# Group statistics of the last image on ScalarE, and three later places in a hand-ordered hypergraph convolution

## The reference

```python
def reference(x, fc_w, fc_b, dist_w, bn_gamma, bn_beta):      # x: (4, 128, 32, 32)
    v = gn(x, G=32, eps=1e-5)                 # group norm: groups of 4 channels, over 4 x 1024 values
    x_flat = v.reshape(B, C, N).transpose(0, 2, 1)            # N = 1024 points of C = 128
    emb = einsum('bnc,ec->bne', x_flat, dist_w)               # 32 wide
    d2 = sq[:, :, None] + sq[:, None, :] - 2.0 * einsum('bne,bme->bnm', emb, emb)
    dist = sqrt(clip(d2, 0.0))
    idx = top_k(-dist, 24)                                    # the 24 nearest points of each point
    adj = knn_mask & (dist <= 10.0) | eye(N)
    X_lin = x_flat @ fc_w.T + fc_b
    Dv, De = sum(adj, axis=2), sum(adj, axis=1)
    out = ((adj / De) @ adj.T / Dv) @ X_lin + x_flat
    o = batch_norm(out) * bn_gamma + bn_beta                  # mean and variance over all four images
    return x + o * sigmoid(o)
```

## Time and profile before

| | |
|---|---|
| median of 3 runs | 178.0 us (177.37 to 181.69) |
| the profiled execution | 177.34 us |
| its span, first to last instruction | 175.6 us |
| granted TensorE clock, mean | 0.97 of 2.4 GHz |
| busy: PE, VectorE, ScalarE, GpSimd | 153.0, 147.6, 108.2, 83.2 us |

### The profile page before, as it was taken

How to read it: one execution, slowest core, us unless ns; L and a number is a source line. 1 busy time by engine, 2 the same in 40 slices (tenths; PEclk the granted TensorE clock), 3 DMA queues, 4 the chain that set the end, 5 groups by cost and what they waited for, 6 DMA issues and landing times.

```text
span 175.6 us, 4086 instructions
## 1 busy us (share of the span) xinstructions
PE 153.0 (87%) x1255; PEld 99.0 (56%) x1257; DVE 147.6 (84%) x888; ACT 108.2 (62%) x200; POOL 83.2 (47%) x104
## 2 busy tenths in 40 slices
PE   7787999979997999899999999999987999998000
PEld 2223543446464772666668746766745888988000
DVE  0667989989999899998999999299989983599782
ACT  1245849999869858995546878257874333090290
POOL 2001309909995745457143989370019575740100
PEclk9999999999999999999999999999999999999855
DMA  6821000043705355046523225391509469600057
GB/s 192 270 92 2 0 2 4 1 52 72 118 7 120 36 90 121 6 95 147 121 37 88 62 63 122 119 93 32 120 0 95 91 181 100 145 4 0 2 201 277
DMA packets 41482, 14.83 MB, mean 84 GB/s; under 512 B 38736, under 2 KB 39656, under 8 KB 41456
## 3 DMA queue, kind: packets, MB, share of 16 engines
q1 hardware_dynamic: 40592, 14.14, 38.3%
q10 hardware_dynamic: 864, 0.40, 1.0%
HBM read 4.02 MB, written 2.13 MB: 35 GB/s over the span
## 4 chain that ended last, share of the span: by engine, by line
PE 67%; ACT 15%; issue 6%; DVE 5%; POOL 4%; ACTq 0%; POOLq 0%; DVEq 0%
PE pt L442 24%; PE pg L412 19%; PE po L467 12%; ACT key L619 4%; ACT H L628 3%; PE po L375 3%; PE pt L495 3%; ACT left L573 2%; PE po L399 2%; POOL wide L759 2%; DVE xn L1080 2%; ACT xn L708 1%; PE po L386 1%; ACT right L579 1%; PE pg L399 1%
## 5 line engine op out<-in xcount | busy, mean ns | idle before, releaser
L867 DVE MAX8 cand<-key 128x8 f32<-128x64 f32 x512 | 81.0, 210 | 1.5 <-ACT key L619 1.2
L442 PEld LDWEIGHTS pt<-xp,H 128*128 128x128 bf16 x768 | 44.4, 97 | 16.3 <-issue 13.9
L442 PE MATMUL pt<-xp,H 128*128 128x128 bf16 (+1 forms) x768 | 48.8, 220 | 0.9 <-DVEq L927 0.6
L759 POOL CAST wide<-HT 128x1024 fp32r<-128x1024 bf16 x31 | 31.4, 1040 | 36.1 <-PE po L467 26.9
L619 ACT ACTIVATE key<-pg 128x512 f32<-128x512 f32 x64 | 34.5, 591 | 22.3 <-PE pg L412 21.9
L412 PE MATMUL pg<-right,left 64*128 64x512 f32 x128 | 41.0, 641 | 4.0 <-ACT key L619 3.1
L628 ACT ACTIVATE H<-key,bound 128x1024 bf16<-128x1024 f32 x32 | 36.8, 1149 | 10.5 <-DVE bound L905 6.8
L467 PE MATMUL po<-wide,tp 128*128 128x512 f32 x96 | 25.4, 406 | 1.6 <-POOL tp L750 1.2
L412 PEld LDWEIGHTS pg<-right,left 64*128 64x128 f32 x128 | 12.7, 184 | 14.7 <-ACT key L619 7.6
L467 PEld LDWEIGHTS po<-wide,tp 128*128 128x128 f32 x96 | 17.1, 189 | 5.6 <-POOL tp L750 1.7
L882 DVE MAX8 top<-cand 128x8 f32<-128x128 f32 x32 | 9.3, 292 | 4.2 <-DVE cand L867 3.1
(11 more groups left out here) (96 smaller groups left out, 170.6 us busy)
## 6 DMA issues: line engine op xcount, KB each, us to landing
dvb<-inv_rows SPq DMA_DIRECT2D x3, 512.0 KB, 4.0
out<-xn SPq DMA_DIRECT2D x6, 256.0 KB, 2.2
x_sb<-x SPq DMA_DIRECT2D x1, 1024.0 KB, 6.2
x_sb<-x SPq DMA_DIRECT2D x1, 512.0 KB, 3.6
HT<-H SPq DMA_TRANSPOSE x32, 2.8
out<-xn SPq DMA_DIRECT2D x4, 128.0 KB, 2.2
x_sb<-x ACTq DMA_DIRECT2D x1, 256.0 KB, 3.2
x_sb<-x SPq DMA_DIRECT2D x1, 256.0 KB, 3.4
```

The source lines that it names most:

```text
L442: mm = pe.matmul(pt[:, j // T_BLOCKS, at:at + wide], lhs, x_cols(b, t, q, wide), start=(t == 0 and j % T_BLOCKS == 0 and q == 0), stop=(t ...
L759: pool.tensor_copy(wide[:, t // TH, :, t % TH * P:(t % TH + 1) * P], HT[:, k % HTS, :, :]).then_inc(s["widened"], 1)
L867: ins = dve.max(cand[:, k % 2, c, :], key[:, k % KEYS, c * CHUNK:(c + 1) * CHUNK])
```

## The change

- VectorE no longer takes image 3's statistics. ACT makes them by running sums: one Copy of the image with a sum, put behind its fourth key drain, and, after the key drain of step 0, one Square with the negative mean as bias and a sum. GpSimd scales the sums to mean and variance (`own_mean`, `own_variance`), three small operations ahead of its loop.
- The group means of images 2 and 3 move on PE from before the loop to step 2 and on VectorE from behind search 0 to behind search 3. The variances move on PE from step 1 to step 4 and on VectorE from behind search 2 to behind search 4; GpSimd's inverse and the normalisation of image 2 move from step 3 to step 4.
- Image 2's tiles 20 to 23 are widened at step 28 and no longer at steps 25 to 27.
- On ACT `operands(b, 1)` stands behind the step's key drain and no longer ahead of it.

```diff
-    [{7: (0, 1), 8: (2, 3), 9: (4, 5), 10: (6,), 11: (7,)}, {6: (0, 1), 7: (2, 3)}]
+    [{7: (0, 1), 8: (2, 3), 12: (4, 5, 6, 7)}, {6: (0, 1), 7: (2, 3)}]
...
@@ tensor engine
-            group_means(2, 2, B)
             keep_busy(3)
...
-                    if k == 1:
+                    if k == 2:
+                        pe.wait_ge(s["own_stat"], 3)
+                        group_means(2, 2, B)
+                    if k == 4:
                         group_variances(2, 2, B)
...
@@ scalar engine
             drain_key(0, 3)
+            act.wait_ge(s["x_in23"], 16)
+            act.activation(work[:, :], x_sb[:, B - 1, :], ACT.Copy, accum_out=own_sum[:, 0:1]).then_inc(s["own_sum"], 1)
             for b in range(B):
...
-                    if k - 2 in EMB_STEPS:
-                        operands(EMB_STEPS[k - 2], 1)
                     if b > 0 and t == SCALE_STEPS[b] + 1:
                         copy_inverse(b - 1)
                     if k + AHEAD < ALL:
                         drain_key((k + AHEAD) // TILES, (k + AHEAD) % TILES)
+                    if k - 2 in EMB_STEPS:
+                        operands(EMB_STEPS[k - 2], 1)
+                    if k == 0:
+                        act.wait_ge(s["own_stat"], 1)
+                        act.wait_ge(s["own_sum"], 1)
+                        act.activation(work[:, :], x_sb[:, B - 1, :], ACT.Square, bias=own_nm[:, :],
+                                       accum_out=own_sum[:, 1:2]).then_inc(s["own_sum"], 1)
...
@@ gpsimd
+            def own_mean(b):
+                pool.wait_ge(s["own_sum"], 1)
+                pool.tensor_scalar(own_nm[:, :], own_sum[:, 0:1], -1.0 / N, None, ALU.mult).then_inc(s["own_stat"], 1)
+                pool.tensor_scalar(gn_mv[:, b, 0:1], own_sum[:, 0:1], 1.0 / N, None, ALU.mult).then_inc(s["own_stat"], 1)
+
+            def own_variance(b):
+                pool.wait_ge(s["own_sum"], 2)
+                pool.tensor_scalar(gn_mv[:, b, 1:2], own_sum[:, 1:2], 1.0 / N, None, ALU.mult).then_inc(s["own_stat"], 1)
...
+            own_mean(B - 1)
+            own_variance(B - 1)
...
-                    if k == 3:
+                    if k == 4:
                         group_inverse()
...
@@ vector engine
-            group_stats(2, 3)
+            third_stats = group_stats(2, 3)
             candidates(0, range(CHUNKS))
             group_inverse(1, 1, 2)
-            dve.wait_ge(s["step"], group_stats(3, B))
-            group_moments(2, B)
+            dve.wait_ge(s["step"], third_stats)
+            group_moments(2, 3)
...
                     search(k)
-                    if k == 0:
+                    if k == 3:
                         group_scale(2, 2, B)
-                    if k == 2:
+                    if k == 4:
                         dve.wait_ge(s["gvar"], 3)
                         dve.tensor_scalar(gn_sd[:, 2:B], g_sums[2][:, B:B + 2], GN_EPS, None, ALU.add).then_inc(s["gvar_in"], 1)
```

More of the change, by code:

```diff
@@ L123, in build @@
         gn_mv = sb("gn_mv", [P, B, 2])
+        own_sum = sb("own_sum", [P, 2])
+        own_nm = sb("own_nm", [P, 1])
         gn_dm = sb("gn_dm", [P, B])
@@ L174, in build @@
         misc = ps("misc", [P, HALF])
-        names = ("const_in d_in w_in x_in0 x_in1 x_in23 out_done setup ones_cols gstat gmean gdm gvar gsd gscale "
+        names = ("const_in d_in w_in x_in0 x_in1 x_in23 out_done setup ones_cols gstat own_stat own_sum gmean gdm gvar gsd gscale "
                  "xn0_ready xn_ready filled drained po_filled po_drained e_sq n_filled l_made r_made norm_out "
```

## The result

The changed kernel is slower: 182.3 us (182.2 to 182.7) against 177.4 to 178.0 for the kernel before beside it, ratio 1.027 with a 95% interval of 1.025 to 1.029. That is outside the forecast range of 176.5 to 180.9. The profiled execution took 182.34 us and its span is 180.5, against 177.34 and 175.6 before, so the traces have to account for 4.9 to 5.0 us.

A forecast was written before the change was run, and what follows sets the result against it. PE and VectorE, both busy, meet at step 13, where VectorE is later by a few tenths. 177.34 + 2.8 (lag) - 0.34 (covered wait) - 0.6 (tail) = 179.2, plus 0.2 gives 179.4 us; range 176.5 to 180.9.

The forecast's parts named there:

- VectorE's gain: VectorE before search 5: two BN_STATS of 1.27 us together leave, but none of the gain outlives a wait.
- the slack of 3.4 us at the flag: Near 113.56 us VectorE waits 3.45 us for PE's flag; this is VectorE's slack and gives PE nothing back.
- the tail: End of kernel: PE's 1.24 us wait for t's low part goes, of which 0.6 us is gained, 0 at worst.
- GpSimd's normalisation of image 2: Comes later with the variances, done about 41.3 us, before the embedding at 44.35 needs it; costed at nothing.
- Step 4 starts when ACT has drained a key tile: PE's step 4, at 36.17 us in the earlier trace: its start was taken to follow ACT's key drain.
- Together 1.16 - 0.88 - 0.28 = 0.0 at best ... I take 0.1: ACT's chain before step 4: Square adds 1.16, left leaves 0.88, means leave 0.28; 0.1 us late taken.
- The release, taken at 1.0 us: VectorE after the variances: adding epsilon and releasing tiles 0 and 1 takes 1.0 us, bounds 0.6 and 1.45.
- my 2.8: Search 5 on VectorE starts 2.8 us late (2.1 to 3.5), and this lag runs on to step 13.
- 0.34 us back: Behind step 13's scatter, PE's 0.34 us wait for ACT's copy of t is covered, leaving PE 2.46 us late.
- the third rival: The stall at step 13 costs PE its clock; scatter and gather take twice as long, 3.65 more, 182.8 us; chance 0.10.
- One pays for the other: Image 2's left behind the drain takes 0.88 of PE's 1.1 us wait; the Square makes PE up to 1.16 late.
- The second rival: VectorE's work sets the pace, so 1.27 us less of it moves all that follows: 175.5 us; chance 0.05.

The follow-up runs named there:

- e3: The kernel before with only the later widening of image 2 in one piece: 176.8 to 177.4 us, ratio 0.997.
- e6: The kernel before with only the moves of means and variances; statistics stay on VectorE, widening and left as before: 180.4 to 181.1 us, ratio 1.018.
- e8: The changed kernel with TensorE's variances in step 3 instead of step 4, the program of e2 run once more: 177.2 to 177.8 us, ratio 1.000.
- e1: The changed kernel with the left operands ahead of ScalarE's key drains again: 180.5 to 183.1 us, ratio 1.025.
- e4: The kernel before with only the left operands moved behind ScalarE's key drains: 176.3 to 176.9 us, ratio 0.994.
- e5: The changed kernel plus 13 filler matmuls on TensorE in step 13, ahead of the scatter: 180.3 to 180.4 us, ratio 1.016.
- e7: The kernel before with left behind the drains and the later widening, without moves or sums on ScalarE: 175.8 us, ratio 0.990.
- e9: e7 plus two small unused tiles that shift the tiles allocated after them: 176.1 to 176.6 us, ratio 0.992 to the kernel before.
- e10: e8 with its two small tiles allocated behind all other tiles, no instruction different: 176.9 to 177.5 us, ratio 0.997 to the kernel before.
- e2: The changed kernel with TensorE's variances in step 3 instead of step 4, first run: 180.3 to 181.7 us, ratio 1.020.

## Why the prediction was wrong

**The place and the mechanism were right.** VectorE's gain did not outlive a wait, though the one that takes it is the wait for the means (1.51 us), which the prediction does not name; the lag comes from the wait for the variances (3.04 us, with TensorE as releaser); it was constant from search 5 to step 13; the slack of 3.4 us at the flag gave nothing back; the tail gave 0.61 in e3 and 0.69 in the changed kernel, forecast 0.6. GpSimd's normalisation of image 2 was in time. e6 and e8 show the wait as the cause: the moves alone bring it, and with the variances one step earlier it is gone.

**The step that failed: "Step 4 starts when ACT has drained a key tile", for which the sum "Together 1.16 - 0.88 - 0.28 = 0.0 at best ... I take 0.1" was made.** The sum is about right for the drain, which came 36.15 - 0.61 - 35.43 = 0.11 later. But the fill of step 4 is the first of image 1 and needs left as well, and left, out of the drain's way, stands behind it: the fill came 37.98 - 0.61 - 36.17 = 1.2 us later, forecast 0.1. For the fill the Square counts in full, 1.15 (the lags of e1 and e6 differ by 1.19), and left gives 0.25 of lag and not 0.88; the order of the two on ScalarE hardly matters to it. I had read its releaser in the earlier trace rows, a drain, and not what else `fill_key` waits for. The means gave 0.13 in e6 (step 4's fill at 36.04, not 36.17), not 0.28. About half of the 1.1 is taken back on the way (the fill finds its key tile drained and takes 1.13 instead of 1.52, and the variances' matmuls start 0.16 before the x fill ends), and VectorE had the variances at 39.74 by the old clock, forecast 39.15.

**The release, taken at 1.0 us, cost 1.36**, near the upper of the two bounds given, in the changed kernel, in e1 and in e6 alike. Both together make the lag 3.72 instead of 2.8. That the moves alone lag by 2.78 is no support for my 2.8: there a smaller delay of TensorE and a longer release add up to it.

**Behind step 13** I gave 0.34 us back. 1.08 come back in truth wherever TensorE is at step 13 over 1 us ahead of VectorE and the clock holds (5.55 to 4.47 in e1, e4, e5, e7): then not only the gather but also the next fill finds ScalarE done. What outweighs them is the third rival's mechanism. TensorE's 3.5 us without work did cost it its clock. The rival's price of 3.65 was too high: the granted clock is 1.00 again from 79 us on, in the middle of the gather, and the price is 6.00 - 4.47 = 1.53. That the time of this rival, 182.8, is near the measured one is no merit of its sum. The Trainium skill (TensorE: Matmul & The Clock Gate, What's actually happening) calls the throttled state the default, which activity releases; the trace agrees (0.50 behind the stall, 1.00 again under scatter and gather), with one thing to add: in e1 TensorE stood 3.23 us and kept its clock, in e6 3.25 us and lost it. So in these two profiles stalls of nearly one length went either way.

**"One pays for the other" held.** e8 has the Square and the moved left, without the late VectorE. TensorE's timeline:

```profile
47.92 1.13 PE L414 MATMUL pg<-right,left 64*128 64x512 f32 x4
...
55.29 1.61 PE L414 MATMUL pg<-right,left 64*128 64x512 f32 x4
```

Less the late start of 0.61, the first of these fills is 1.00 later than before (46.31), and the second, behind image 2's left, is level (54.68 against 54.65). What I did not see is the other side: without the Square, in e4 and e7, left's gain stays and becomes the lead that is worth 1.0 us at step 13. In the changed kernel this can't be seen, because the Square takes the lead, and a late VectorE removes the same waits.

**The second rival**, that less work on VectorE sets the pace, and the rule of the Trainium skill beside it (Perfetto Trace Analysis, Identifying the Most-Contended Engine), are tested by no run here: in the change and in e8 alike VectorE's relief ends at the wait for the means, and in e8 search 5 begins where it did before (37.94 - 0.61 against 37.38). What the runs show is what the move costs elsewhere: e8 is where the kernel before was, while e7 has the full statistics on VectorE and is 1.9 us faster than e8. In the profiles 0.5 of the 1.9 is the start, 0.7 is step 13 (5.21 against 4.48: in e8 TensorE arrives when VectorE does, and still waits 0.56 us for ScalarE's copy of t), and 0.65 is the last output.

**What no step had**: 0.65 for the last output and 0.2 for VectorE's last operations. The forecast lay 2.9 below the result: 0.9 from the lag, 0.8 from step 13, 0.85 from these two and 0.4 from the start (0.61, of which I had added 0.2), less 0.1 that the tail gave more.

## What to carry over

Before crediting an operation that moves out of the way of a waiting instruction, list everything that this instruction waits for, not just the releaser that the profile names: the second condition may be hardly earlier. A wait that is put into a queue that never waits should be checked step by step along the queue it waits for, since one place earlier on TensorE was worth 4.6 us here. Time that one engine gains is worth something only where it becomes a lead at the place where the queues meet: left's gain near 54 us paid 1.0 us in e4 and nothing in e8, where the Square had used it up. A change with several parts is worth cutting up: two of these three were gains (1.0 and 0.55 us), hidden under the third, and e7, which keeps only them, is the kernel to use.

## What the runs showed of the hardware

Two small tiles that shift H and HT by 64 bytes in each partition make the DMA transposes take 3.2 instead of 2.8 us (e9 against e7, e8 against e10). GpSimd's widening waits for them, 11.1 us in all in e9 and 9.7 in e7, but the interval at step 13 stays (4.47 and 4.48), so no time of the kernel is put down to this. The last output takes 3.1 instead of 2.46 us in the kernels with the longer program (the changed kernel, e1, e2, e5, e8, e10). In the trace's packets of the queue of kind "instruction", the last 8192-byte packet lies at 178.6 of 180.5 us in the changed kernel, beside that output, and at 166.8 of 175.6 before; the other runs divide in the same way. That instruction loading delays the output is thus likely, but no run changed the program's length alone.
